# Row maxima turned as two half-array matmuls in two PSUM banks, wherever score rows or network matmuls stand, instead of by one whole-array transpose

## What is computed

```python
xn = _layernorm(x, axis=-1)
s = _L0_attn_ref(xn, w_qkv, b_qkv, w_out, b_out)      # 16 heads of 16
g = _silu(_L0_ffn_ref(xn, k0, k1, k2, s0, s1, s2))    # 256 -> 1024 -> 1024 -> 256, weights +1 or -1
x = x + s * g
```

## Time and profile before

| | us |
|---|---|
| median of 3 runs | 2318.76 |
| lowest, highest | 2318.16, 2321.8 |
| the profiled execution | 2317.55 |
| its span, first to last instruction | 2315.8 |
| TensorE busy | 2230.2 (96%) |
| VectorE busy | 1811.5 (78%) |
| ScalarE busy | 1580.9 (68%) |
| GpSimdE busy | 915.3 (40%) |
| granted TensorE clock, mean | 0.986 |

### The profile page before, as it was taken

One profiled execution on the slowest core, in us unless ns is written; L12 is line 12 of the kernel. 1 busy time (PEld: TensorE's weight loads), 2 busy tenths in 40 slices (PEclk: granted clock), 3 DMA queues, 4 the chain that ended last, 5 costly groups with the idle time before them and its releaser, 6 DMA issues.

```text
span 2315.8 us, 60916 instructions
## 1 busy us (share of the span) xinstructions
PE 2230.2 (96%) x23760; PEld 1539.8 (66%) x23760; DVE 1811.5 (78%) x4516; ACT 1580.9 (68%) x3199; POOL 915.3 (40%) x1080
## 2 busy tenths in 40 slices
PE   7997999999999999999999999999999999999985
PEld 6786776666666666677666666666666666666652
DVE  7774787888888878788888878788888787888722
ACT  5662466777777777777777677677777776776662
POOL 1003534333433534344453445343443544354433
PEclk9998999999999999999999999999999999999997
DMA  8984111111111313131121223131322212132221
GB/s 299 359 317 167 39 29 40 43 50 46 47 49 35 94 40 87 48 86 51 51 83 45 81 59 83 41 90 43 83 55 53 83 44 84 50 83 69 81 92 58
DMA packets 157844, 193.31 MB, mean 83 GB/s; under 512 B 65276, under 2 KB 102076, under 8 KB 157560
## 3 DMA queue, kind: packets, MB, share of 16 engines
q1 hardware_dynamic: 156600, 189.41, 27.2%
q10 hardware_dynamic: 960, 0.00, 0.0%
HBM read 112.13 MB, written 76.14 MB: 81 GB/s over the span
## 4 chain that ended last, share of the span: by engine, by line
PE 84%; DMA 6%; DVE 4%; SPq 2%; issue 1%; ACT 1%; POOL 1%; POOLq 0%; ACTq 0%; DVEq 0%
PE b_ps L1406 25%; PE b_pv_ps L1372 22%; PE b_ps L1343 15%; PE b_ps L1353 12%; PE b_ps L1402 5%; DMA a_xs<-L_attn_x 4%; PE b_ps L1427 3%; DVE a_stats L397 1%; DVE a_qk_parts L435 1%; ACT b_u L1492 1%; DVE b_part_max L1518 1%; SPq L113 1%; PE b_ps L1360 1%; SPq L1186 0%; PE a_qk_ps L291 0%
## 5 line engine op out<-in xcount | busy, mean ns | idle before, releaser
L1461 ACT ACTIVATE b_probs<-b_ps 128x512 f32<-128x512 f32 (+3 forms) x2560 | 1258.4, 538 | 563.8 <-PE b_ps L1343 533.7
L1518 DVE TENSOR_REDUCE b_part_max<-b_ps 128x1 f32<-128x512 f32 x1536 | 972.4, 681 | 184.0 <-PE b_ps L1353 177.2
L1353 PE MATMUL b_ps<-k_kst,k_qst 48*128 48x512 f32 (+3 forms) x2560 | 896.3, 391 | 8.7 <-DMA k_kst<-qk_parts 3.4
L1343 PE MATMUL b_ps<-k_qst,k_kst 50*128 50x512 f32 (+3 forms) x2560 | 891.7, 389 | 11.7 <-DMA k_qst<-b_max_parts 11.1
L1343 PEld LDWEIGHTS b_ps<-k_qst,k_kst 50*128 50x128 f32 x2560 | 431.9, 185 | 323.7 <-DVE b_part_max L1518 115.8
L1515 DVE CUSTOM_DVE_ANT_0 b_ps<-b_ps,k_mask 128x512 f32<-128x512 f32 (+3 forms) x1024 | 483.5, 513 | 153.8 <-PE b_ps L1353 147.1
L1372 PE MATMUL b_pv_ps<-b_probs,k_vst 128*32 128x512 f32 (+3 forms) x5120 | 597.5, 541 | 0.5 <-POOL b_probs L1247 0.2
L1406 PE MATMUL b_ps<-b_u_hi,k_w 64*128 64x256 f32 x4096 | 590.0, 281 | 2.1 <-ACT b_u L1492 1.1
L1406 PE MATMUL b_ps<-b_u_lo,k_w 64*128 64x256 f32 x4096 | 588.5, 280 | 0.0
L1353 PEld LDWEIGHTS b_ps<-k_kst,k_qst 48*128 48x128 f32 x2560 | 432.9, 185 | 137.6 <-DVE b_part_max L1518 43.5
L1406 PEld LDWEIGHTS b_ps<-b_u_hi,k_w 64*128 64x128 f32 x4096 | 460.7, 187 | 20.2 <-ACT b_z L1483 4.2
(11 more groups left out here) (105 smaller groups left out, 1922.6 us busy)
## 6 DMA issues: line engine op xcount, KB each, us to landing
qk_parts<-a_qk_parts SPq DMA_DIRECT2D x64, 512.0 KB, 3.9
k_kst<-qk_parts SPq DMA_DIRECT2D x384, 64.0 KB, 2.3
k_qst<-qk_parts SPq DMA_DIRECT2D x384, 64.0 KB, 2.3
a_xs<-L_attn_x SPq DMA_DIRECT2D x16, 512.0 KB, 6.0
xn_T<-a_xT SPq DMA_DIRECT2D x16, 512.0 KB, 5.7
v_plain<-a_v_out SPq DMA_DIRECT2D x16, 512.0 KB, 5.4
k_xf<-xn_T SPq DMA_DIRECT2D x32, 256.0 KB, 3.2
b_v_in<-v_plain SPq DMA_DIRECT2D x64, 128.0 KB, 2.6
```

What stands on the lines that cost most here:

```text
L1343: pe.matmul(dst[:, 0:cols], keys, qst[rows, c, pair, 0:cols], start=True, stop=True).then_inc(s_ready, 1)
L1353: pe.matmul(dst[:, 0:CHUNK - k1], qst[rows, c, pair, i * P:(i + 1) * P], kst[rows, k_slot(kc, g % 2), pair, k1:CHUNK], start=True, stop=Tr ...
L1461: act.activation(probs[:, s % P_SLOTS, h, 0:cols], ps[:, banks[place, 0][0], 0:cols], ACT.Exp, scale=HD ** -0.5).then_inc(exp_done, 1)
L1518: dve.tensor_reduce(dst, src, AX_X, ALU.max).then_inc(ring_read, 1)
```

## The change

The turn leaves the whole-array mode. A new `turn_maxima()` emits it in mode R, when two ring banks are free, one turn a call. It is called after every step of `made()` unless the mode is V, and in `wait()`; the change between V and the other modes no longer emits turns, nor does a fetch.

TensorE's transpose becomes two plain float32 matmuls with the identity, on rows 0 to 63 and 64 to 127 of `neg_max`, each on its half of the array and into a bank of its own. VectorE has a copy and a subtract of 16x64 for each half, four instructions in place of two, and SyncE waits for both. The four DMAs stay.

```diff
-    def whole_array(self):
-        while self.turns and self.turns[0][2] <= self.clock["PE"]:
+    def turn_maxima(self):
+        if self.turns and self.turns[0][2] <= self.clock["PE"] and self.free("ring", HALVES) <= self.clock["PE"]:
             n, c, _ = self.turns.pop(0)
             self.end_span()
-            self.enter("W")
+            self.enter("R")
             at = self.emit("negmax", n, c)
-            bank = self.take((at, 0), "ring")
-            self.whole(0.08)
-            self.release[bank] = self.reads("DVE", self.clock["PE"], self.MAX, 400)
+            for half in range(HALVES):
+                bank = self.take((at, half), "ring")
+                done = self.on_tile(half, 0.12)
+                self.release[bank] = self.reads("DVE", done, self.MAX, 400)
             self.rows_at[n, c] = self.release[bank] + 4.5
+
+    def whole_array(self):
         while self.due:
...
         self.end_span()
+        self.turn_maxima()
         self.whole_array()
...
             self.beside(self.step())
+            if self.mode != "V":
+                self.turn_maxima()
             kind = self.choose()
...
                     g, c = arg
-                    uses += 1
+                    uses += HALVES
                     sp.wait_ge(ring_read, uses)
...
-                    dst = claimed((place, 0))
+                    dst = [claimed((place, half)) for half in range(HALVES)]
                     pe.wait_ge(padded, 1)
                     pe.wait_ge(neg_done, g * CPB + chunk_of(c) + 1)
-                    pe.transpose(dst[:, 0:P], neg_max[:], identity[:]).then_inc(ring_ready, 1)
+                    for half in range(HALVES):
+                        rows = slice(half * HALF, (half + 1) * HALF)
+                        pe.matmul(dst[half][:, 0:HALF], neg_max[rows], identity[rows, rows], start=True, stop=True
+                                  ).then_inc(ring_ready, 1)
...
-                    src = filled((place, 0))[0:NROWS, 0:P]
                     if at > 0:
                         dve.wait_ge(max_rows, at * ROWS * DMA)
-                    dve.tensor_copy(max_parts[:, HI, :], src).then_inc(max_high, 1)
-                    dve.wait_ge(max_high, at + 1)
-                    dve.tensor_tensor(max_parts[:, LO, :], src, max_parts[:, HI, :].bitcast(F32),
-                                      ALU.subtract).then_inc(ring_read, 1)
+                    for half in range(HALVES):
+                        src = filled((place, half))[0:NROWS, 0:HALF]
+                        cols = slice(half * HALF, (half + 1) * HALF)
+                        dve.tensor_copy(max_parts[:, HI, cols], src).then_inc(max_high, 1)
+                        dve.wait_ge(max_high, at * HALVES + half + 1)
+                        dve.tensor_tensor(max_parts[:, LO, cols], src, max_parts[:, HI, cols].bitcast(F32),
+                                          ALU.subtract).then_inc(ring_read, 1)
```

## The result

| | before | after |
|---|---|---|
| median, us | 2318.57 | 2390.97 |
| lowest, highest | 2318.16, 2321.8 | 2388.59, 2393.72 |
| the profiled execution | 2317.55 | 2390.99 |
| ratio after : before | | 1.031 (95% interval 1.0293 to 1.0326) |

The change costs 72 us. The forecast was par, 2316.8, and its range ended at 2327. The rows of the kernel after have moved by a few lines: S is L1350, M L1360, the turn L1369, PV L1382, network L1412 and L1416, projection L1437, maxima L1525 and L1528, `neg` L1532, copy and subtract L1543 and L1545.

The account below looks back on a forecast made before the run. PE was taken to bound the kernel from 330 to 2250 us. PE's 14.1 - 17.3 = -3.2, plus DVE's 0.2 and 1.0, gave -2.0: 2317.55 to 2315.6, median 2316.8 us; range 2309.5 to 2327.

Parts of the forecast that it names:

- The step that failed: Ring banks: a turn holds two of five for some 1.5 us where it held one; network fills, priced at nothing.
- Rival E: Planner's order: moving 64 entries shifts the greedy plan; one stall of some 4 us goes or doubles, 2313 or 2321; chance 0.05.
- I price it by the starts of matmuls: PE's timeline: a turn costs what it takes from PE's order; removing the old turns saves 17.3 us.
- a forecast of 0.22: New turn on PE: two records per half at 0.11 each, set by weight loads; 0.22 a turn, 14.1 us over 64.
- halves which end up there have the same price: Borders: if the halves end up there again, they stand at the end of R at the forecast's price.
- The rule on drains: Mode changes on PE: by the skill's rule leaving mode W saves a drain every turn; forecast that it mostly doesn't.
- the prediction's prices of 0.46 for a transpose and 0.22 for the halves: Turns on PE: old ones among rows or network 0.46 each with both mode changes, six such; new ones 0.22.
- forecast 20: DVE's work: two pairs at 0.45 replace one at 0.59, +0.31 a turn, +20 us over the kernel.
- +1.2: DVE's share on the path: +0.2 for 60 turns from 330 to 2250 us, +1.0 for three at the start.
- A's own range: Par case, 2316.8, chance 0.50: 2313 to 2322, with up to a quarter of DVE's 20 us coming through.
- Hardly on the chain: DVE from 330 to 2250 us: busy 81% but hardly on the chain, so +0.2 for all 60 turns.
- D, the turn too early: PE's wait on `neg_done` and two banks: 0.3 for half of the turns, 9.6 us, 2326.4; chance 0.17.

Follow-up runs that it names:

- an unrelated constant: Kernel before with the planner told that the rows of a turn are due 3.5 us after it, not 4.5; no instruction changed: 2369.16 us, 1.0207.
- the stops of `sums_T`: Changed kernel with the network's allowance at 200 pairs instead of 60 and round RRRRV instead of RRFRRV, one `sums_T` buffer: 2371.36 us, 1.0217.
- the first experiment: Changed kernel's order and two claimed banks, but with the whole-array transpose and two VectorE instructions of before: 2399.8 us, 1.0347.
- the allowance of 400: Changed kernel with the network's allowance at 400 instead of 60, the round as it was, and two `sums_T` buffers: 2368.11 us, 1.0206.

## Why the prediction was wrong

**The step that failed** is "The planner takes them only when both are free and fills with network, whose total is fixed, so I put this at nothing". The first part is true. But that the network's total is fixed does not put it at hand when two banks of five are held: it may run only 60 pairs ahead of its share, and its own two banks may still be read. The plan has 500 waits in place of 122, 206 of them at the limit and 292 with the network not ready. The second bank was worth +51 us at the new place and +21 at the old one. I had the code of `choose` before me and the earlier trace rows as the price of a failed fill, and did not ask whether filler was at hand at the moment of the turn, only whether its total was fixed.

**The case that came true, mis-sized.** Rival E said that the greedy plan may move much else, and then priced it by one visible stall at 4 us with a chance of 0.05. The place alone was worth +29.5, and an unrelated constant +49. Where an order is computed, this rival is no remainder: it was the one thing in the change that could be worked out beforehand, by running the planner (+67 for the changed kernel by its own clock, +72 measured). That clock is a guide and no more: it gave +39 for the constant that measured +49, +16 for the one-bank turn that measured +29.5, and -1.5 where the stops of `sums_T`, for which it has no clock, made +51.

**"I price it by the starts of matmuls"** holds for the turn and misses what surrounds it. Over all 64 turns, from the first record of a turn to the next start is 16.2 us or 0.25 a turn, against a forecast of 0.22. Three of them from the timeline of PE:

```profile
450.69 0.34 PE L1369 MATMUL b_ps<-k_identity,b_neg_max 64*128 64x64 f32 x4
450.83 0.37 PE L1416 MATMUL b_ps<-b_u_lo,k_w 64*128 64x256 f32 x2
...
704.20 0.43 PE L1369 MATMUL b_ps<-k_identity,b_neg_max 64*128 64x64 f32 x4
704.56 1.06 PE L1382 MATMUL b_pv_ps<-b_probs,k_vst 128*32 128x512 f32 x8
705.55 0.49 PE L1350 MATMUL b_ps<-k_qst,k_kst 50*128 50x512 f32 x1
...
845.62 0.44 PE L1369 MATMUL b_ps<-k_identity,b_neg_max 64*128 64x64 f32 x4
845.84 0.40 PE L1416 MATMUL b_ps<-b_u_hi,k_w 64*128 64x256 f32 x2
```

0.14 and 0.22 among network, 0.36 with the border behind it. The PV at the border still takes 0.99, as the 1.00 of the earlier trace rows. The 0.14 is not the whole price, for part of it is paid one matmul later, as the earlier trace rows had shown. One and the same turn, with the halves and then, in the first experiment, with the transpose:

```profile
1093.11 0.28 PE L1416 MATMUL b_ps<-b_u_hi,k_w 64*128 64x256 f32 x2
1093.23 0.33 PE L1369 MATMUL b_ps<-k_identity,b_neg_max 64*128 64x64 f32 x4
1093.37 0.37 PE L1416 MATMUL b_ps<-b_u_lo,k_w 64*128 64x256 f32 x2
1093.57 0.28 PE L1416 MATMUL b_ps<-b_u_hi,k_w 64*128 64x256 f32 x2
1093.69 0.28 PE L1416 MATMUL b_ps<-b_u_lo,k_w 64*128 64x256 f32 x2
...
1095.18 0.28 PE L1414 MATMUL b_ps<-b_u_hi,k_w 64*128 64x256 f32 x2
1095.39 0.33 PE L1368 MATMUL b_ps<-k_identity,b_neg_max 128*128 128x128 f32 x1
1095.65 0.39 PE L1414 MATMUL b_ps<-b_u_lo,k_w 64*128 64x256 f32 x2
1095.88 0.28 PE L1414 MATMUL b_ps<-b_u_hi,k_w 64*128 64x256 f32 x2
1095.99 0.28 PE L1414 MATMUL b_ps<-b_u_lo,k_w 64*128 64x256 f32 x2
```

Undisturbed, network pairs start 0.118 apart. Counted from the network start ahead of the turn to the third one behind it, less three such steps, this turn cost 0.23 with the halves and 0.46 with the transpose. Four turns of this order have two network pairs ahead and four behind; counted so, they took 0.22 to 0.26 with the halves and 0.46 to 0.51 with the transpose, 0.23 and 0.48 in the mean.
At a border it was not. The prediction said that halves which end up there have the same price. Where they do (the run with halves at the old place), 36 of them stand before a PV, at 0.37 each, where the transpose took 0.26:

```profile
701.92 0.34 PE L1410 MATMUL b_ps<-b_u_hi,k_w 64*128 64x256 f32 x2
702.22 0.44 PE L1363 MATMUL b_ps<-k_identity,b_neg_max 64*128 64x64 f32 x4
702.59 1.07 PE L1376 MATMUL b_pv_ps<-b_probs,k_vst 128*32 128x512 f32 x8
```

36 x 0.11 = 4 us and DVE's 5.3 make about the 8 us by which that run lies above the one with two banks and transposes. Why the halves hold the border for longer was not tested. In the changed kernel only five turns stand before a PV.

**The rule on drains.** At the borders leaving mode W saved nothing. Among network it does: the prediction's prices of 0.46 for a transpose and 0.22 for the halves are near what the rows above show. 64 times this difference would be 15 us, less DVE's 5.3: 10, an estimate from above, since not all turns stand there; measured in the same order were 8. The Trainium skill ("TensorEngine Tiling (Array Packing)", Key Properties) has it that a change of tiling mode drains the engine. The trace agrees in part: the network matmul ahead of a transpose holds the array for 0.21 and the one behind it for 0.23 in place of 0.12. But the one behind the halves, where no mode changes, takes 0.20 too, so only the 0.09 ahead is seen to go with the mode.

**DVE** was mis-sized: its busy time rose by 13.9 us in all (forecast 20), but in the run that changes DVE alone +5.3 in place of +1.2 reached the end, which A's own range had allowed for (a quarter of the 20). "Hardly on the chain" hid that DVE holds the ring banks.

**D, the turn too early**, was there only in small. Before all L1369 PE sat idle for 0.7 us in sum. But 18 turns start just 0.147 behind the end of `neg`, so they waited for it, and the weight load ahead of them stood idle for 1.9 us in sum. In the eight with two network pairs ahead these took some 0.16 longer than at the usual pace; if that is the wait, it is about 3 us for the 18 (an estimate, not tested).

The new place's +29.5 is not divided further. One bank in whole-array mode at the same place cost 13 only, and its transposes stand among rows and network as well (all 64; here 63), so their drains are in both. The plans differ: 127 waits and never at the network's limit there, 253 waits and 68 at the limit here. That makes the order the likelier source of the remaining 17, but no run parts them. Open too is why the stops of `sums_T` spared the kernel before.

## What to carry to other kernels

When a list scheduler writes the order, run it for both versions and compare its end and its idle steps before pricing a single instruction; count how often its filler is not at hand (at its limit, or short of banks of its own), for a filler whose total is fixed is free only while it can be moved. And compare versions under the planner's constants that suit each, for an edit that looks like the cost of an operation may be that of an order. A buffer held for longer is paid by whoever needs the same pool: ask it of each added bank, even one that nobody writes. And when all engines of the changed kernel look as busy as before, count instructions in a fixed window: fewer in the same time on every engine pointed at the order here. The count alone doesn't settle it: with the allowance of 400 it was above that of before, and the kernel was still 2% slower.

## What the runs showed of the hardware

A busy share of 99% of PE went with 15884, 16369 and 16663 matmuls in the same 1470 us at a granted clock of 1.00; a row matmul alone on its half of the array counted as busy for 0.47 of the 0.75 us that it had (653.48). Two float32 matmuls of 64 columns, one on each half of the array and two records each, cost 0.23 us among network matmuls (mean of four turns) and 0.37 ahead of a PV (36 turns); a whole-array 128x128 float32 transpose cost 0.48 and 0.26 in these two places. Nine DMAs issued one after the other held SyncE's queue for 5.1 us (2.75 for the four stores of the maxima, 1.83 and 0.55 for the five of the sums), and with one shared buffer behind them PE stopped 11 times for some 3 us; a second buffer took all 11 away. Behind 8 of these stops the granted clock was 0.50 for 3.4 or 6.8 us.
